# Graph attention kernel, second edge layer: queries expanded ahead of the sums, older sums added at the end of each step

## What is computed

```python
q = (h[rows] @ Wq.T + bq).reshape(-1, 8, 16)      # rows: the edge's source list, sums go there
k = (h[cols] @ Wk.T + bk).reshape(-1, 8, 16)
v = (h[cols] @ Wv.T + bv).reshape(-1, 8, 16)
att = einsum('ehd,ehd->eh', q, k) / sqrt(16)
exp_att = exp(clip(att, -10.0, 10.0))
att_sum = segment_sum(exp_att, rows)
out = segment_sum(exp_att[..., None] / (att_sum[rows] + 1e-08) * v, rows)
x = x + layernorm(out + h) * gamma + beta
```

## Time and profile before

| | us |
|---|---|
| timed, median of 3 runs (2272.0 to 2273.41) | 2273.32 |
| profiled execution, span | 2940.6 |
| PE busy in it | 1840.2 (63%) |
| DVE busy | 1874.7 (64%) |
| ACT busy | 1279.6 (44%) |
| POOL busy | 1551.0 (53%) |

### The profile page before, as it was taken

The page is one execution under the profiler, slowest core; times in us unless marked ns, Lnnn a source line. Parts: engine busy times, 40 slices in busy tenths (PEclk is TensorE's granted clock), DMA queues, the critical chain, the costliest instruction groups (busy, mean ns, idle before and its releaser), DMA issues. The chain is left out here.

```text
span 2940.6 us, 44304 instructions
## 1 busy us (share of the span) xinstructions
PE 1840.2 (63%) x10257; PEld 1461.4 (50%) x10258; DVE 1874.7 (64%) x5089; ACT 1279.6 (44%) x3362; POOL 1551.0 (53%) x1594
## 2 busy tenths in 40 slices
PE   5323346767576676677776767676666676666662
PEld 4323334544344444344454656566556665656662
DVE  9858775655455755455775666666666666666666
ACT  8524345755465565556653323333223332322333
POOL 0256655665556565565434555545455555555544
PEclk7756667877778787878887888888888888888886
DMA  3211111111111111111116444445444544444453
GB/s 105 62 41 42 43 39 39 45 42 38 38 38 45 38 41 41 39 44 39 33 68 185 126 125 127 127 122 131 119 121 124 132 123 122 125 123 123 126 122 55
DMA packets 234145, 244.06 MB, mean 83 GB/s; under 512 B 32925, under 2 KB 195229, under 8 KB 233989
## 3 DMA queue, kind: packets, MB, share of 16 engines
q0 software_dynamic: 61136, 147.00, 18.5%
q1 hardware_dynamic: 142357, 81.55, 10.8%
q10 hardware_dynamic: 30624, 15.21, 2.2%
HBM read 225.01 MB, written 18.62 MB: 83 GB/s over the span
## 5 line engine op out<-in xcount | busy, mean ns | idle before, releaser
L303 POOL DMA_INDIRECT rows<-y_tab,idx x832 | 795.6, 956 | 589.8 <-issue 307.9
L1340 POOL DMA_INDIRECT x<-kv_tab,kv_idx x672 | 682.7, 1016 | 623.0 <-DVE msg L1392 403.9
L1563 PE MATMUL ps_kv<-kv_s,hot_low 128*128 x1362 | 406.0, 443 | 168.9 <-DVE hot_low L1364 90.0
L780 ACT ACTIVATE sort_v<-sort_t,staged,minus 128x128 f16<-128x128 f16 x914 | 360.7, 480 | 309.1 <-remote 243.1
L872 PE MATMUL ps_sort<-sort_hi,sort_v 128*128 128x496 f16 x1662 | 417.6, 403 | 117.3 <-issue 112.4
L619 DVE TENSOR_SCALAR sort_v<-iota_h,staged 128x128 f16<-128x128 f16 x748 | 243.2, 325 | 339.2 <-remote 269.0
L1550 PE MATMUL ps_m<-msg,x 128*128 128x136 f32 x1792 | 295.4, 315 | 243.4 <-DVE msg L1392 182.7
L830 PE MATMUL ps_sum<-rows,hot 128*128 128x128 f32 x1664 | 282.0, 323 | 250.3 <-issue 120.1
L1374 DVE TENSOR_TENSOR by_tile<-ps_q,x 128x512 f32<-128x512 f32 x224 | 154.5, 690 | 404.9 <-remote 257.4
L830 PEld LDWEIGHTS ps_sum<-rows,hot 128*128 128x128 f32 x1664 | 260.4, 235 | 271.8 <-issue 139.4
L1550 PEld LDWEIGHTS ps_m<-msg,x 128*128 128x128 f32 x1792 | 263.3, 219 | 263.1 <-issue 245.7
(11 more groups left out here) (290 smaller groups left out, 2072.2 us busy)
## 6 DMA issues: line engine op xcount, KB each, us to landing
weights<-tile_tab SPq DMA_DIRECT2D x114, 256.0 KB
x<-tile_tab SPq DMA_DIRECT2D x113, 256.0 KB
weights<-tile_tab ACTq DMA_DIRECT2D x58, 256.0 KB
rows<-y_tab,idx POOLq DMA_INDIRECT x832
x<-kv_tab,kv_idx POOLq DMA_INDIRECT x672
kv_tab<-kv_s SPq DMA_DIRECT2D x12, 512.0 KB
x<-x_in SPq DMA_DIRECT2D x1, 3328.0 KB, 13.3
out<-x SPq DMA_DIRECT2D x12, 256.0 KB
```

Source lines behind the costliest of these rows:

```text
L303: pool.indirect_dma_start(out=rows[:, k * SPAN + n, :], out_offset=None, in_=y_tab, in_offset=bass.IndirectOffsetOnAxis(ap=idx[:, k, n:n + ...
L780: last = nc.scalar.activation(to[:, k % 2, m, :], sort_t[:, k % 2, m, :], ACT.Relu, bias=staged[:, v, c:c + 1], scale=minus[:, v, c:c + 1])
L1340: pool.indirect_dma_start(out=rows[:, u, k, :], out_offset=None, in_=kv_tab, in_offset=bass.IndirectOffsetOnAxis(ap=idx[:, u, k:k + 1], ax ...
L1563: last = nc.tensor.matmul(ps_kv[:, k % 2, :], hot_low[:, w, k * P:(k + 1) * P], kv_s[:, ds(low + w, 1), :], start=w == 0, stop=w == WINDOW ...
```

## The change

TensorE's step becomes `expand(u+2)`, `sums(u)`, `fill(u+3)`. VectorE's step becomes V, P, O (now for the quad one ahead), S, the window one-hots in quad 2, add 0, c, adds 1 to 3. The one-hots of a second quad ahead of the first pass go, and those of a quad in the tail. SyncE's last three loads, behind its loop, wait on a register that is bounded from below (`wait_positive`, which exists in the kernel: a register operation, the wait and a no-op).

```diff
@@ -1314,9 +1314,9 @@
 
             @block.sync
             def _(sp):
-                def load_src(i, u):
-
-                    sp.wait_ge(off_made, i * QUADS + u + 1)
+                def load_src(i, u, after=sp.wait_ge):
+
+                    after(off_made, i * QUADS + u + 1)
                     first = i * FETCHED + u * QUAD if u < QUADS - 1 else ST + i * QUAD
                     sp.dma_start(from_src[u % 2].rearrange("p (k d) -> p k d", k=QUAD),
                                  tile_tab[ds(first, QUAD), 0:P].unsqueeze(0).to_broadcast([P, QUAD, P])).then_inc(src_in[u % 2], 16)
@@ -1326,7 +1326,7 @@
                     for u in range(QUADS):
                         load_src(i, u)
                 for u in range(QUADS - 1):
-                    load_src(passes, u)
+                    load_src(passes, u, lambda semaphore, value: wait_positive(sp, semaphore, value))
 
             @block.gpsimd
             def _(pool):
@@ -1425,16 +1425,15 @@
                             values(i, u - 1)
                         elif begun:
                             values(i - 1, QUADS - 1)
-                        tile_sums(0)
                         products(i, u)
-                        tile_sums(1)
+                        one_hot(i if u < QUADS - 1 else i + 1, (u + 1) % QUADS)
+                        scores(i, u)
                         if u == 2:
                             hots_of_low(i + 1)
-                        scores(i, u)
-                        tile_sums(2)
+                        tile_sums(0)
                         clip(i, u)
-                        one_hot(i if u < 2 else i + 1, (u + 2) % QUADS)
-                        tile_sums(3)
+                        for k in range(1, QUAD):
+                            tile_sums(k)
 
                 nc.vector.tensor_scalar(minus_lane[:, :], lane[:, :], -1.0, -1.0, ALU.mult, ALU.add).then_inc(lane_set, 1)
                 then(nc.vector.tensor_scalar(lanes[:, :], iota[:, 0:WINDOWS], float(P), lane[:, :], ALU.mult, ALU.add))
@@ -1443,7 +1442,6 @@
                     last = nc.vector.tensor_scalar(hot_low[:, w, :], from_low, lanes[:, w:w + 1], None, ALU.is_equal)
                 last.then_inc(hot_low_ready, 1)
                 one_hot(0, 0)
-                one_hot(0, 1)
                 run_pass(0, False)
                 with v.If(passes_of(mybir.EngineType.DVE) > 1):
                     passes = passes_of(mybir.EngineType.DVE)
@@ -1456,8 +1454,6 @@
                 values(end, QUADS - 1)
                 for k in range(QUAD):
                     add_sums(end, 2, k, buckets[k])
-
-                one_hot(end + 1, 2)
                 for k in range(QUAD):
                     add_sums(end, 3, k, buckets[QUAD + k])
                 v.wait_ge(low_in, (end + 3) * 16)
@@ -1572,9 +1568,9 @@
                 with pe.Fori(0, passes_of(mybir.EngineType.PE)) as i:
                     ahead = of_pass(mybir.EngineType.PE, i + 1, slice(0, GROUP + QUAD))
                     for u in range(QUADS):
+                        expand(i if u < 2 else i + 1, (u + 2) % QUADS, ahead[u * QUAD:(u + 1) * QUAD])
                         sums(i, u)
                         fill(i if u < 1 else i + 1, (u + 3) % QUADS, ahead[GROUP + u])
-                        expand(i if u < 2 else i + 1, (u + 2) % QUADS, ahead[u * QUAD:(u + 1) * QUAD])
 
 
         with ExitStack() as c5, nc.Block() as block:
```

## The result

The changed kernel takes 2372.08 us (median of 4 runs, 2371.87 to 2373.62) against 2272.7 us before. The ratio is 1.0436, 95% interval 1.0424 to 1.0449. The forecast was 2406 us with a range of 2300 to 2440.

The account below looks back on a forecast made before the run. VectorE's instruction order was taken to bound the second edge layer. To the timed 2273.3 us came 135 (adds) + 24 (boundaries) - 1 (small parts) = 158, less 25 of waits: 2406 us, range 2300 to 2440.

Parts of the forecast that it names:

- Sign and mechanism: Second edge layer: kernel slower by 133 us, bound by VectorE with a step of 3.92 us; chance 0.80.
- the sum: Second layer: 18.2 us a pass against 15.3; extra 158 us less 25 us of waits gives +133 us.
- The price of the adds and the boundary: VectorE's second layer: adds 0.44 us apart instead of 0.20, 135 us; later start of each next pass, 24 us.
- VectorE's busy total: Sign expected in the profile after: VectorE's own busy time stays near 1875 us.
- The waits given back: TensorE's expansion first ends the products' waits for queries in the second layer: 25 us, between 0 and 51.
- the account: Timed run before: 301.6 us rest, 1040 first layer, 881 second make 2222.6 of 2273.3; some 51 us for waits.
- Hold-ups of the recording: Profiled run's 667 us excess read as waits the recording brings; profiled span after expected at about 2800 us.
- Rival B: Products' profiled waits are real in the timed run; with half of 404.5 us real, about 2230 us; chance 0.11.
- C: Rival: VectorE's grouped adds cost nothing, staying 0.20 us apart; about 2271 us; chance 0.05.
- D: Rival: TensorE idles more, stays at 1.2 GHz longer and becomes the bound; 2507 us at 60%; chance 0.04.

Follow-up runs that it names:

- the pair without the gathers' bound: One of twelve gathers a pass left out, in the old kernel with TensorE's new order and in the changed kernel: 2212.1 and 2372.4 us.
- bounded_wait: The kernel before with only SyncE's last three waits bounded: 2275.3 us, ratio 0.9999.
- the second recording: New recording of the kernel before with only SyncE's last three waits bounded: span 2275.4 us; the first recording's was 2940.6 us.
- vector_only: The changed kernel with TensorE's three calls back in their old order (sums, fill, expand): 2497.0 us, ratio 1.0974.
- tensor_only: The kernel before with TensorE's new order (expand, sums, fill) and SyncE's bounded wait, VectorE as before: 2241.9 us, ratio 0.9851.

## Why the prediction was right, point by point

**Sign and mechanism: right.** VectorE is the bound, the step is 3.92 us, the products wait for nobody; the pass takes 18.4 us (1023.2 us over 55.75 passes) against the 18.2 us of the sum.

**The price of the adds and the boundary: right.** The sum had 135 + 24 - 1 = 158 us for VectorE; the pair without the gathers' bound measures 158 us in the layer. The spacing read from the tail holds in the loop (0.44 us), and the boundary went from 46.2 to 70.6 us, 24 us as forecast. The Trainium skill, VectorE: DVE Perf Modes, section "The DRAIN you can't avoid", has eight copies take as long with a semaphore after each as with one after the last. What it would suggest for this part, no price, these runs don't bear out for short adds that each wait for the one before: 2372.1 against 2241.6 us for their place alone. No run took the wait itself away. Each add also takes its bucket's row number from a register, and that this has no part in the 0.44 us is not shown.

**VectorE's busy total: a sign that did not come.** It was to stay near 1875 us and is 1928.4 us (1877.1 in bounded_wait). The operations are the same; it is the lost overlap of the adds, about 0.09 us for each of three adds in 222 steps, an estimate of 60 us. The sum had this within its spacing of 0.44 us, so the time was not touched.

**The waits given back: too small, and this is the error of 34 us.** The step took 25 us between bounds of 0 and 51. The kernel before loses 62.6 us between its first and last products (924.7 us in the recording of bounded_wait, whose stage stands below, against 862.1 us at VectorE's own pace), so 158 - 63 = 95 us are left; measured were 1023.2 - 924.7 = 98.5 us in the layer and 99.4 in time.

```profile
1288.50:2213.20 924.70, 742.52 (x4902) 677.43 (x4901) 824.38 (x2169) 395.30 (x951) 709.07 (x665) 0.99 0.66 173
```

Its idle entries name 38.9 us of queries and 9.9 us of rows. Most of the remainder is again counted as busy (824.38 against 812.78 us, 11.6 us), since a wait also undoes the 0.09 us by which neighbours overlap. What the step had wrong is the chain it looked at: it compared 4.11 us with 4.10 us in a step without window one-hots, and in the recording of bounded_wait quad 3 waits in every pass, behind fills that wait for these one-hots. The upper bound of 51 us was itself too low, because the account took 301.6 us for the rest of the program from the disturbed recording, where it is 285.0; with that it is 67 us. The account's method held: both layers could be placed within 10 us of what they are (1040 against 1050, 932 at most against 940.4) with a recording that was 667 us too long.

**Hold-ups of the recording: right, with a wrong consequence.** They were of the recording, as the second one shows. But I expected the profiled span after to carry most of them as well, about 2800 us; it was 2370.4 us. They don't come with a kernel, and a forecast of a profiled span from one disturbed recording has no basis. What makes them can't be told from these runs; the Trainium skill, NOTIFIC — the notification-queue block, section 7.1, has a mechanism that fits, a full queue that stalls the engine that writes to it, and no run here shows it.

**Rival B** (real waits of over 158 us) falls with the second recording and the 63 us, C with the adds' spacing, D with the layer's granted clock of 0.94 and no wait for TensorE. But D was near in another place: holding the clock up gave vector_only 87 us back.

**Where the two parts belong together.** The prediction gave each part one price. They have two: TensorE's order is worth 32 us beside VectorE's old order (2274.1 - 2241.9) and 125 us beside its new one (2497.0 - 2372.1). VectorE's order costs 130 us beside TensorE's new order and 223 us beside the old one. I had worked out that a longer step hides TensorE's old chain (4.11 us against 4.52) and did not carry through that the same longer step gives TensorE idle time at the boundary, after which it ran at 1.2 GHz.

## What to carry to other kernels

Operations that wait for their own predecessor on the same engine are cheap only with other work between them: 0.20 us became 0.44 us each when they were put together. Before reading a profile's waits, set its span against the timed runs; where it is far longer, add up floors of the stages from busy time and issue rates, and bound the real waits by what is left. Freeing a wait is worth at most the distance to the next engine's pace: here TensorE's order freed the queries and the gathers of GpSimd kept half of it.

## What the runs showed of the hardware that was not expected

- Extra work made a kernel faster: 64 small bf16 matmuls a pass, whose results nobody reads, took 2497.0 to 2410.0 us, since TensorE otherwise idled at the loop boundary (2.43 us in the pass shown) and ran the following 3.4 us at a granted 0.50.
- A gather keeps GpSimd busy for 0.95 us, with 0.30 us ahead of it, but some take 1.15 to 1.58 us (mean 1.02 us in tensor_only), and in a kernel that they bound the mean counts.
- One recording held up the whole program by 667 us while VectorE's and ScalarE's busy times agree with a clean one (1874.7 against 1877.1 us, 1279.6 against 1278.5 us). TensorE's is longer in it, 1840.2 against 1624.6 us, at a granted clock of 0.85 against 0.99 in the second layer.
